# Layer 1 of a two-layer recurrent model: its weights and the attention product moved into the expert stage, a chunk's gated rows quantised as one stream, the recurrence one chunk at a time with tokens on partitions

## The reference

```python
x = L0_attn_X
xn = _layernorm(x, axis=-1)
s = _L0_attn_ref(xn, L0_attn_W_qkv, L0_attn_W_out)
g = _silu(_L0_ffn_ref(xn, ...))       # 8 experts, top 2, and a shared expert
x = x + s * g
xn = _layernorm(x, axis=-1)
s = _L1_attn_ref(xn, ...)             # rmsnorm, x @ Bmat, a decaying recurrence over t, @ C, + D
g = _silu(_L1_ffn_ref(xn, L1_ffn_w_gate, L1_ffn_w_up, L1_ffn_w_down))
x = x + s * g
```

```python
scale = jnp.max(jnp.abs(xb), axis=-1, keepdims=True) / 6.0
scale = jnp.maximum(scale, jnp.float32(1e-12))
q = _GRID[searchsorted(_MID, jnp.abs(xb / scale))] * jnp.sign(xb) * scale
gate = fp4_linear(x, w_gate); y = fp4_linear(x, w_up)      # 128 -> 352
h = silu(gate) * y
return fp4_linear(h, w_down)                                # 352 -> 128
```

## Time and profile before

| what | us |
|---|---|
| median of three runs | 1974.12 |
| lowest, highest | 1966.82, 1975.07 |
| the profiled execution | 1962.93 |
| its span | 1960.8 |
| PE busy over the span | 1828.6 |
| DVE busy over the span | 1506.1 |
| POOL busy over the span | 1424.2 |
| ACT busy over the span | 1012.8 |

### The profile page before, as it was taken

How to read it: one execution, slowest core, us unless ns; L and a number is a source line. 1 busy time by engine, 2 the same in 40 slices (tenths; PEclk the granted TensorE clock), 3 DMA queues, 4 the chain that set the end, 5 groups by cost and what they waited for, 6 DMA issues and landing times. The chain is left out here.

```text
span 1960.8 us, 33201 instructions
## 1 busy us (share of the span) xinstructions
PE 1828.6 (93%) x10425; PEld 1045.9 (53%) x10425; DVE 1506.1 (77%) x2045; ACT 1012.8 (52%) x1513; POOL 1424.2 (73%) x862
## 2 busy tenths in 40 slices
PE   6899999999999999999999999999998799965776
PEld 5455555555555555555555555555554688753345
DVE  5877777777777777777777777777777688787776
ACT  4345544454454455444544544554544588754543
POOL 3388888888888888888888888888887166636453
PEclk9899999999999999999999999999999799986899
DMA  6101010110101010101101010101010677230000
GB/s 219 45 12 55 19 54 21 43 46 19 54 11 54 11 55 19 54 21 43 45 21 54 11 54 11 55 19 54 21 43 21 216 246 243 79 92 19 0 17 27
DMA packets 98115, 107.82 MB, mean 55 GB/s; under 512 B 8224, under 2 KB 88032, under 8 KB 94880
## 3 DMA queue, kind: packets, MB, share of 16 engines
q1 hardware_dynamic: 93088, 97.15, 15.1%
q0 software_dynamic: 4992, 10.27, 1.5%
HBM read 52.56 MB, written 26.82 MB: 40 GB/s over the span
## 5 line engine op out<-in xcount | busy, mean ns | idle before, releaser
L1154 POOL TENSOR_TENSOR psum_k<-psum_k,probs 128x1024 f32<-128x1024 f32 x384 | 925.5, 2410 | 199.2 <-ACT probs L1099 184.2
L1171 DVE TENSOR_REDUCE mxh<-ps_m 128x2 f32<-128x1024 f32 x518 | 633.5, 1223 | 255.0 <-PE ps_m L931 253.4
L1099 ACT ACTIVATE probs<-ps_s 128x1024 f32<-128x1024 f32 x512 | 497.4, 1023 | 264.0 <-PE ps_s L948 212.8
L956 PE MATMUL ps_v<-probs,V 128*64 128x512 f32 x2056 | 489.8, 597 | 0.0
L1195 DVE RECIPROCAL rden<-den 128x128 f32<-128x128 f32 x260 | 245.6, 946 | 25.2 <-ACT den L1068 16.0
L956 PEld LDWEIGHTS ps_v<-probs,V 128*64 128x64 f32 x2056 | 137.2, 137 | 235.9 <-issue 233.4
L931 PE MATMUL ps_m<-k_hi,q_hi 64*128 64x512 f32 x1036 | 237.8, 452 | 11.1 <-DVE mxh L1171 7.2
L946 PE MATMUL ps_s<-q_lo,k_hi 64*128 64x512 f32 x1024 | 202.8, 389 | 0.0
L948 PE MATMUL ps_s<-shift,ones_r 64*128 64x512 f32 x1024 | 202.7, 388 | 0.0
L946 PE MATMUL ps_s<-q_hi,k_lo 64*128 64x512 f32 x1024 | 202.2, 389 | 0.0
L946 PE MATMUL ps_s<-q_hi,k_hi 64*128 64x512 f32 x1024 | 202.0, 390 | 0.0
(11 more groups left out here) (317 smaller groups left out, 2840.7 us busy)
## 6 DMA issues: line engine op xcount, KB each, us to landing
e_ew<-w_split SPq DMA_DIRECT2D x23, 1024.0 KB, 7.3
V<-V_next SPq DMA_DIRECT2D x33, 512.0 KB, 3.3
xs_hi<-xh SPq DMA_DIRECT2D x16, 512.0 KB, 3.7
xs_lo<-xl SPq DMA_DIRECT2D x16, 512.0 KB, 4.3
rows<-in_blank_d SPq DMA_DIRECT2D x4, 1483.5 KB, 18.6
e_x_raw<-rows SPq DMA_DIRECT2D x23, 258.0 KB, 3.5
we_raw<-in_experts_d SPq DMA_DIRECT2D x33, 128.0 KB, 2.4
w_split<-we_hi SPq DMA_DIRECT2D x32, 128.0 KB, 1.8
```

The source lines that it names most:

```text
L956: ins = nc.tensor.matmul(ps_v[rows, :], V[par][:, kt, rows], probs[:, t % RING, x, :], start=kt == 0, stop=kt == KT - 1)
L1099: nc.scalar.activation(probs[:, t % RING, :, :], ps_s[t % 2][:, :, :], ACT.Exp, scale=SCALE).then_inc(p_done, 1)
L1154: nc.gpsimd.tensor_tensor(acc, probs[:, (t - 1) % RING, :, :] if kt == 1 else acc, probs[:, t % RING, :, :], ALU.add).then_inc(add_done, 1)
L1171: nc.vector.tensor_reduce(mxh[:, kh, t, :], max_bank(unit, i)[:, :, :], AX.X, ALU.max).then_inc(m_done, 1)
```

## The change

It touches the expert stage and layer 1.

1. SP loads the shared expert's weights after the rows and weights of all first four tiles, and then layer 1's three weight tensors, into memory that the summed rows use later. ACT and DVE split the shared weights at tiles 1 and 2, inside the loops.
2. Layer 1's weights are quantised in the expert stage: steps on DVE at blocks 9 to 12, absolute values on ACT at tile 3, four passes over each tensor on POOL ahead of its first store. PE transposes them at tiles 23 to 25, ACT copies them. `layer1_early` holds the results over both stages.
3. The attention rows are transposed per chunk at tiles 27 and on, with ACT's Silu and DVE's product beside them. The first two batches of X are loaded into the stored rows' memory.
4. Layer 1 starts from there: no attended rows, no weights. The input streams of chunks 0 and 1 are quantised one after the other, and moments(3) comes after chunk 0's products.
5. `body(c)` quantises all four token tiles of chunk c (1408 columns) as one stream, interleaved with the input rows of chunk c+3; the scratch is doubled.
6. The recurrence's product is done one chunk per body with the states as the stationary operand, so that it comes out with tokens on partitions; D is added by a product of a row of ones with a row. The down product is turned round as well. The last addition of x is one pass of POOL (DVE for chunk 7) in place of products with the identity and ACT's copy.

```diff
             weights(0, 0)
             rows(0, 1)
             weights(0, 1)
-            sp.dma_start(ws_raw[:, :], g.inp["shared_d"]).then_inc(ws_in, 16)
             for s in range(2, NS):
                 rows(0, s)
                 weights(0, s)
+            sp.dma_start(ws_raw[:, :], g.inp["shared_d"]).then_inc(ws_in, 16)
+            for k, src in enumerate((g.inp["w_gate_d"], g.inp["w_up_d"])):
+                for j, (lo, n) in enumerate(IB):
+                    sp.dma_start(w_gu[0:n, 3 * k + j, :], src[lo:lo + n, :]).then_inc(w1_in, 16)
+            sp.dma_start(w_dn, g.inp["w_down_d"]).then_inc(w1_in, 16)
             with sp.Fori(*LOOP) as i:
                 for s in range(NS):
                     rows(i, s)
@@ -420,7 +466,13 @@
                 weights(*divmod(u, NS))
             for s in range(NS):
                 sp.wait_ge(y_out[s], 64 * len(range(s, ROUTED, NS)))
-            for v in range(NCH):
+            sp.wait_ge(w1T_ready, 3)
+            sums(0)
+            sums(1)
+            for v in range(4):
+                x = g.inp["X"][v // 2][v % 2 * CH:(v % 2 + 1) * CH, :]
+                sp.dma_start(y_row[v][:, :, :], x.rearrange("(n p) d -> p n d", p=P)).then_inc(g.x_early[v], 16)
+            for v in range(2, NCH):
                 sums(v)
...
+                        if j == 2 and chunk_at(i, s, 0) in (0, 1, 2):
+                            layer1_weights(chunk_at(i, s, 0))
+                        if j == 1 and chunk_at(i, s, 4) is not None:
+                            attended(chunk_at(i, s, 4))
...
+            for v in range(EARLY_A - 1, NCH):
+                attended(v)
             token_rows(*rows.pop(0))
...
+                        if j == 3 and isinstance(i, int) and at(i, s) == 1:
+                            shared_high()
+                        if j == 2 and isinstance(i, int) and at(i, s) == 3:
+                            layer1_sizes()
+                        if j == 3 and chunk_at(i, s, 0) in (0, 1, 2):
+                            layer1_weights(chunk_at(i, s, 0))
+                        if j == 0 and chunk_at(i, s, 4) is not None:
+                            gate(chunk_at(i, s, 4))
...
             turns(act, body)
             for i, q in tail(SPLIT, NB):
                 high(i, q)
-            for i, s in tail(2, NS):
+            gate(NCH - 4)
+            for k, (i, s) in enumerate(tail(2, NS)):
                 result(i, s)
-            for v in range(NCH):
-                gate(v)
+                if k == 0:
+                    gate(NCH - 3)
+            gate(NCH - 2)
+            gate(NCH - 1)
```

POOL's part of the early weights, DVE's steps in the loop, and layer 1:

```diff
+            def scaled(k):
+
+                val, m = W1[k]
+                n = 3 * k
+                nb = val.shape[1] // BLK
+                pool.wait_ge(w1_size, k + 1)
+                nc.gpsimd.tensor_scalar(m, m, 1.5, MAGIC, ALU.max, ALU.mult).then_inc(w1_grid, 1)
+                pool.wait_ge(w1_grid, n + 1)
+                nc.gpsimd.tensor_tensor(val, val, m, ALU.add).then_inc(w1_grid, 1)
+                pool.wait_ge(w1_grid, n + 2)
+                nc.gpsimd.tensor_tensor(val, val, m, ALU.subtract).then_inc(w1_grid, 1)
+                pool.wait_ge(w1_grid, n + 3)
+                val = val.rearrange("p (n k) -> p n k", k=BLK)
+                nc.gpsimd.tensor_tensor(val, val, w_s[k][:, :].unsqueeze(2).to_broadcast([P, nb, BLK]), ALU.mult).then_inc(w1_done, 1)
+
+            scaled(0)
+            scaled(1)
...
+                        if isinstance(i, int) and at(i, s) == 2 and j == 0:
+                            shared_low()
+                        if isinstance(i, int) and 0 <= at(i, s) * FT + j - 9 < 4:
+                            layer1_weights(at(i, s) * FT + j - 9)
+                        if j == 2 and chunk_at(i, s, 4) is not None:
+                            gated(chunk_at(i, s, 4))
...
+            quantised_input(0, QS, 0)
+            quantised_input(1, 2 * QS, 1, q_x12[0])
             inverses(2)
-            quantised_input(2, 5 * QS, 4, q_x12[1])
+            quantised_input(2, 3 * QS, 2, q_x12[1])
             inverses(3)
+
+            def finish(c):
+                pool.wait_ge(pr2_done, c + 1)
+                pool.wait_ge(stored, c * 16 + 1)
+                nc.gpsimd.tensor_tensor(out_t[:, :, :], pr2[:, :].rearrange("p (t d) -> p t d", d=D),
+                                        x1[:, c * TC:(c + 1) * TC, :], ALU.add).then_inc(o_done, 1)
...
+                if not no_result(c):
+                    finish(c - 2)
                 if not first(c):
                     pool.wait_ge(hT_ready, c)
-                for i, end in enumerate((A_END,) if last(c) else (A_END, 2 * QL if no_input(c) else B_END)):
-                    pool.wait_ge(q_step, steps_before(c) + end)
-                    scaled(hq[:, i * HT:(i + 1) * HT, :].rearrange("p t (n k) -> p (t n) k", k=BLK), q_h[i],
-                           n + i).then_inc(hq_done, 1)
+                pool.wait_ge(q_step, steps_before(c) + (QL if no_input(c) else H_END))
+                t = HT if last(c) else TC
+                scaled(hq[:, 0:t, :].rearrange("p t (n k) -> p (t n) k", k=BLK), tuple(a[:, 0:t * NBI] for a in q_h[c % 2]),
+                       n).then_inc(hq_done, 1)
                 if not no_input(c):
-                    quantised_input(c + 3, steps_before(c) + X_END, n + 2)
+                    quantised_input(c + 3, steps_before(c) + X_END, n + 1)
...
             normed_T(0)
+            input_T(0)
+            gates(0, 0)
             state_inputs(0)
-            input_T(0)
-            weights()
-            gates(0, 0)
...
-                sizes(q_h[0], steps_before(c) + 4)
-                if c == 2:
-                    recurrence(0)
-                if c == 5:
-                    recurrence(1)
+                def sizes_of_rest():
+                    if no_input(c):
+                        sizes(q_h[c % 2], steps_before(c) + 4)
+                    else:
+                        sizes(q_h[c % 2], steps_before(c) + 7)
+                        sizes(q_x, steps_before(c) + 8)
+
                 if c in (1, 3):
                     normed_T((c + 3) // 2)
                 if not last(c):
                     gates(c + 1, 1)
                 if c in (1, 3):
                     state_inputs((c + 3) // 2)
+                if c in (0, 1, 3):
+                    sizes_of_rest()
                 if first(c):
                     normalise(2)
                 else:
                     hidden_T(c - 1)
                 if not no_hidden(c):
                     input_T(c + 2)
-                if no_input(c):
-                    sizes(q_h[1], steps_before(c) + QL + 4)
-                else:
-                    sizes(q_h[1], steps_before(c) + QL + 7)
-                    sizes(q_x, steps_before(c) + QL + 8)
+                if c not in (0, 1, 3):
+                    sizes_of_rest()
                 if not no_hidden(c):
                     gates(c + 2, 0)
                 if not first(c):
                     gate(c - 1)
-                if not no_result(c):
-                    finish(c - 2)
+                    recurrence(c - 1)
...
-                v.wait_ge(x_in[b], 16)
-                v.wait_ge(prT_ready, b + 1)
-                if b >= 2:
+                gate = g.gate[:, b * T:(b + 1) * T]
+                if b < 2:
+                    for k in range(HALF):
+                        part = slice(k * CH, (k + 1) * CH)
+                        v.wait_ge(g.x_early[b * HALF + k], 16)
+                        ins = nc.vector.tensor_tensor(x[:, part], gate[:, part], g.y_row[b * HALF + k][:, :, :].rearrange("p t d -> p (t d)"), ALU.add)
+                else:
+                    v.wait_ge(x_in[b], 16)
                     v.wait_ge(rstd_step, RS * (b - 2) + 4)
-                gate = g.gate[:, b * T:(b + 1) * T]
-                step(nc.vector.tensor_tensor(gate, (ps_a, ps_b)[b % 2][:, :], gate, ALU.mult))
-                nc.vector.tensor_tensor(x, gate, x, ALU.add).then_inc(x1_done, 1)
+                    ins = nc.vector.tensor_tensor(x, gate, x, ALU.add)
+                ins.then_inc(x1_done, 1)
...
+            quantise(nc, v, q_step, 0, [(input_rows(0), *(a[:] for a in q_x))])
+            quantise(nc, v, q_step, QS, [(input_rows(1), *q_x12[0])])
             moments(2)
-            moments(3)
             hidden(0, 0)
             hidden(0, 1)
             v.wait_ge(xn_done, 2)
-            quantise(nc, v, q_step, 4 * QS, [(input_rows(2), *q_x12[1])])
+            quantise(nc, v, q_step, 2 * QS, [(input_rows(2), *q_x12[1])])
             hidden(0, 2)
             hidden(0, 3)
+            moments(3)
...
-                streams = [hB] if no_input(c) else [hB, (input_rows(c + 3), *(a[:] for a in q_x))]
+                streams = [(h[:, c % 2, :, :].rearrange("p t (n k) -> p (t n) k", k=BLK), *(a[:] for a in q_h[c % 2]))]
+                if not no_input(c):
+                    streams.append((input_rows(c + 3), *(a[:] for a in q_x)))
```

(52 more changed lines are left out.)

306 lines of the change are left out of this document (138 added, 168 removed).

## The result

The changed kernel takes 2006.12 us (median of 4 runs, 2002.13 to 2008.07); the kernel before took 1970.47 in the four runs beside it, the three given ahead and one more. Ratio 1.0172, 95% interval 1.0153 to 1.0192: **some 35 us slower, where 1943.4, 31 us faster, was forecast.** The profiled execution took 2002.13 us with a span of 2000.3, 39.5 more than the 1960.8 before.

A forecast was written before the change was run, and what follows sets the result against it. PE was taken to pace the expert stage, a chain hopping DVE, POOL, PE and ACT to bound layer 1. 8.6 - 18.7 - 18.6 - 2.0 = -30.7, from 1974.12 to 1943.4 us; range 1928 to 1964.

The forecast's parts named there:

- until chunk 1: Layer 1 from its start to chunk 1: 51.5 us against 70.2, -18.7 (bounds -12 and -22).
- the end: Chunk 7 and the end of layer 1: 26.7 us against 28.75, -2.0.
- signs of being wrong: Wrong if expert tile distances don't move, chunks stay at 17 us, or the loop's clock drops below 0.7.
- A chunk: Layer 1, chunks 1 to 6: 88.7 us with gaps, against 107.28, -18.6 (bounds 0 and -24).
- The first rival: Chunks don't shorten, since one 1408-column stream can't overlap itself and POOL's 5.5 us shows each turn: -12, 1962; chance 0.14.
- one per chunk behind the down product: Chunk loop: four recurrences in one burst become one per chunk, six of 0.60, as many columns as before; the loop's gain.
- the fourth rival: Slower: PE falls to 1.2 GHz through the loop, its work barely changing; 135 us against 107.28, net +16, 1990; chance 0.05.
- (b): Expert stage: layer 1's early weights add DVE steps and 9.1 us of POOL passes; +8.5 (bounds 0 and 14).
- (a): Expert stage: moving the shared weights' load removes PE's 2.99 us wait and part of the slow clock; -4.5 (bounds -3, -5.5).
- (c): Expert stage: nine transposes for weights on a full PE; +0.9.
- (d): Expert stage: attention rows and gates move here; +2.4 and +1.3, gates 0, and 0 for table swaps around the added Silu.
- Where Abs comes first (1 and 3) DVE alone binds: Layer 1, chunks 1 and 3: DVE alone sets 11.7 and 13.7 us; chunk 3 adds the scan, 3.5.

The follow-up runs named there:

- e8: Kernel after without any work by DVE, ACT or POOL on the two early weights (loads, transposes, copies stay): 1977.15 us, ratio 1.0066 to the kernel before.
- e13: Kernel after with two input scratches, no early weight work and no row of ones: 1940.67 us, ratio 0.9867 to the kernel before.
- e9: Kernel after with two input scratches, POOL's passes spread, D in one product a chunk, absolute values before the copy in chunks 1 and 3: 1966.03 us, ratio 0.9959.

## Why the prediction was wrong

By stretches the profiled execution missed the forecast by 70.2 us: 16.7 up to the start of layer 1 (1.6 of it ahead of the expert stage), until chunk 1 4.3, chunks 1 to 6 33.4, the end 15.8. One of its own signs of being wrong came: chunks 1 to 6 took 16.1 to 24.3 us each.

- **Failed: "A chunk", where the chunk was built up from DVE's first reduction, with "POOL's two passes over the last chunk to 5.7" beside it.** It took for granted that this reduction starts beside those passes. The diff's chunk start waits for `xq_done` of the last chunk, behind all four. The first rival had priced just this (POOL's passes "show in full in each turn"), but only as no gain. Measured 25.3 us of waits; the second scratch took 19.4 us out of layer 1, 8.2 of it in chunks 1 to 6.
- **Failed: the recurrence, "one per chunk behind the down product", counted as no more work than before.** With the row of ones a chunk's recurrence took 3.4 us on PE, against 1.0 before and 1.16 without the row, and the end has two of them at the lower clock, 11.6 us. Leaving the row out took 20.8 us out of layer 1 (24 by the ratios). "Its work barely changes", in the fourth rival, was the same slip.
- **Mis-sized: (b), +8.5 with an upper bound of 14.** Tile time 162.3 against 138.3 without the work: 24. POOL's passes, priced by those of layer 1, 1.49 us for 768 columns, and forecast at 9.1 in all, took 15; DVE's steps took 3.9, where 3.4 was forecast. The second pass ran from 1560.73 to 1562.83, and a square of DVE that started in it ended only at 1563.38: after 2.34 us, where its like with no pass beside it take 0.68. That agrees with the Trainium skill, SBUF — State Buffer (SBUF: two separate sides), by which whichever of the two starts first has the port pair for its whole instruction. On chip 9 the two parts by themselves made 8.6, the forecast, but by luck: POOL's passes were longer than priced and cost less than their time. What the rest of the 24 is stays open, as said above: the passes in a row, or what makes ACT wait on chips 3 and 5.
- **Right: (a).** -4.5 forecast; with no early weight work the tile time fell from 143.0 to 138.3, -4.7, and the wait of 2.99 us is gone.
- **Right to about 1 us: (c) and (d) together.** +4.6 forecast; from the last routed tile to the start of layer 1 it took 86.0 us before and in e8, to the first residual sum, 89.7. The zero for swapped tables held: after has one table load in the stage, at 1733.8, though Silu stands between Relus from there on.
- **Right: until chunk 1,** once the wait ahead of it is out: 51.1 in e13, 51.5 forecast.
- **Failed: what is left of the chunks.** With every found cause out, chunks 1 to 6 still took 14.3 us over the forecast, and only 4.3 less than before, where the gain looked for was 18.6. 11.8 of the 14.3 are in chunks 1 and 3, for which the forecast had "Where Abs comes first (1 and 3) DVE alone binds": there ACT copies the recurrence inputs first, and the scan takes 4.9 us, not 3.5. But in e9, which turned ACT's order round, what chunks 1 and 3 gained the chunks behind them lost, and DVE's wait for the absolute values is 24.0 us in e13, against 12.7 before. So the order is not the whole of it, and what is stays open.
- **The end** was nearly right but for the row of ones: 28.3 in e13, 26.7 forecast.
- The fourth rival, slower by the clock, named the right sign for another reason: the loop's grant fell only from 0.91 to 0.82. In the end it did matter, 0.53.
